# Values of layer 1 weighed three key tiles at a time behind every sixth pair, with sixteen weight buffers

## What is computed

```python
q, k, v = proj(wq, bq), proj(wk, bk), proj(wv, bv)
scores = einsum("bhqd,bhkd->bhqk", q, k) / sqrt(16) + spatial_bias_matrix
attn = softmax(scores, axis=-1)
ctx = einsum("bhqk,bhkd->bhqd", attn, v)
resid = ctx.reshape(B, S, 128) @ wo + bo + x_seq
out = layernorm(resid) * ln_gamma + ln_beta
```

## Time and profile before

| | |
|---|---|
| median of 3 runs | 10369.0 us (10361.93 to 10372.07) |
| profiled execution, its own time | 10373.9 us |
| its span | 10372.1 us |
| TensorE matmul busy | 9606.5 us, 93% |
| VectorE busy | 7181.1 us, 69% |
| ScalarE busy | 5674.1 us, 55% |
| GpSimd busy | 963.2 us, 9% |

### The profile page before, as it was taken

One profiled execution on the slowest core, in us unless ns is written; L12 is line 12 of the kernel. 1 busy time (PEld: TensorE's weight loads), 2 busy tenths in 40 slices (PEclk: granted clock), 3 DMA queues, 4 the chain that ended last, 5 costly groups with the idle time before them and its releaser, 6 DMA issues.

```text
span 10372.1 us, 345836 instructions
## 1 busy us (share of the span) xinstructions
PE 9606.5 (93%) x139471; PEld 4590.9 (44%) x139471; DVE 7181.1 (69%) x24584; ACT 5674.1 (55%) x11896; POOL 963.2 (9%) x862
## 2 busy tenths in 40 slices
PE   7888851699999999999999999999999999999998
PEld 4444430244444444444444444444444444444444
DVE  3555540577777777777777777777777777777774
ACT  1111100266666666666666666666666666666665
POOL 0222220100100010001000100011001100110001
PEclk8888875699999999999999999999999999999999
DMA  2444434100110011001100110011001100110000
GB/s 54 86 85 87 85 85 31 49 10 16 35 29 11 14 36 31 11 14 36 32 10 14 34 34 9 15 31 34 11 15 30 29 17 13 33 28 19 10 13 15
DMA packets 443040, 324.25 MB, mean 31 GB/s; under 512 B 75495, under 2 KB 436424, under 8 KB 440520
## 3 DMA queue, kind: packets, MB, share of 16 engines
q1 hardware_dynamic: 433988, 299.91, 12.5%
q10 hardware_dynamic: 7488, 2.77, 0.5%
HBM read 197.66 MB, written 104.87 MB: 29 GB/s over the span
## 4 chain that ended last, share of the span: by engine, by line
PE 75%; ACT 3%; DMA 2%; SPq 1%; issue 1%; DVE 0%; POOL 0%; ACTq 0%; POOLq 0%; DVEq 0%
PE l_ps L1006 51%; PE l_ps L1084 22%; ACT p L1187 2%; DMA sums_scratch<-ctx_raw 1%; PE l_ps L1099 1%; PE l_ps L1115 1%; ACT rows L1179 1%; PE l_ps L1116 0%; PE l_ps L1102 0%; SPq L842 0%; DMA sums<-sums_scratch 0%; PE l_ps L1096 0%; SPq L837 0%; SPq L830 0%; DMA stacks_scratch<-parts 0%
## 5 line engine op out<-in xcount | busy, mean ns | idle before, releaser
L1187 ACT ACTIVATE p<-l_ps 128x448 f32<-128x448 f32 x10976 | 5263.9, 543 | 2691.4 <-PE l_ps L1006 2683.9
L1228 DVE CUSTOM_DVE_ANT_0 summed<-l_ps,pair_bias 128x448 f16<-128x448 f32 x9408 | 5379.8, 619 | 1792.0 <-PE l_ps L1006 1776.2
L1006 PE MATMUL l_ps<-ks,qs 64*64 64x448 f16 x21952 | 3925.8, 355 | 59.3 <-DVE partial L1228 35.0
L1006 PE MATMUL l_ps<-high,id 64*64 64x448 f16 x21952 | 3928.9, 354 | 27.6 <-ACT p L1187 3.0
L1006 PE MATMUL l_ps<-qs,ks 64*64 64x448 f16 x21952 | 3922.7, 354 | 0.0
L1006 PE MATMUL l_ps<-low,id 64*64 64x448 f16 x21952 | 3902.4, 352 | 0.7 <-issue 0.7
L1006 PE MATMUL l_ps<-rows,pick_row 64*64 64x448 f16 x21952 | 3874.2, 349 | 0.0
L1084 PE MATMUL l_ps<-p,v 128*32 128x448 f32 x22400 | 2413.9, 547 | 0.0
L1006 PEld LDWEIGHTS l_ps<-high,id 64*64 64x64 f16 x21952 | 1204.1, 106 | 1493.8 <-issue 981.0
L1006 PEld LDWEIGHTS l_ps<-ks,qs 64*64 64x64 f16 x21952 | 1204.1, 106 | 877.0 <-DVE partial L1228 573.6
L1006 PEld LDWEIGHTS l_ps<-qs,ks 64*64 64x64 f16 x21952 | 1205.6, 106 | 394.0 <-issue 0.4
(11 more groups left out here) (130 smaller groups left out, 4285.7 us busy)
## 6 DMA issues: line engine op xcount, KB each, us to landing
stacks_scratch<-parts SPq DMA_DIRECT2D x448, 112.0 KB
x<-in_x SPq DMA_DIRECT2D x16, 1568.0 KB
ks<-stacks_scratch SPq DMA_DIRECT2D x32, 784.0 KB, 9.6
qs<-stacks_scratch SPq DMA_DIRECT2D x224, 112.0 KB, 2.8
recip<-inverse_scratch SPq DMA_DIRECT2D x448, 56.0 KB, 2.0
h_scratch<-x SPq DMA_DIRECT2D x8, 1568.0 KB
w_scratch<-x SPq DMA_DIRECT2D x8, 1568.0 KB
mh<-h_scratch SPq DMA_DIRECT2D x64, 196.0 KB
```

The costliest lines, as they stand in the source:

```text
L1006: last = nc.tensor.matmul(ps[h * BT:(h + 1) * BT, bank, 0:CH], lhs(part, h), rhs(part, h), start=start, stop=True, skip_group_check=not start)
L1187: nc.scalar.activation(p[unit % PB][:], ps[:, bank_of(unit), 0:CH], ACT.Exp).then_inc(exp_done, 1)
L1228: nc.vector.tensor_tensor_reduce(summed[unit % 2][:], ps[:, AB + unit % MAXIMA, 0:CH], bias.rearrange("p s t -> p (s t)"), 1.0, LOWEST, AL ...
```

## The change

`PB` goes from 12 to 16, and `weighed_at` names other pairs: three key tiles behind pairs 7, 13, 19, ... 43 and behind pair 0 of the next tile, and the last key tile behind pair 2 as before. The products, the exponentials, the maxima and the DMAs are the same in number and in shape.

```diff
-        PB = 12
+        PB = 16
...
             if i == 0 and n >= 1:
-                return [(n - 1, 22), (n - 1, 23)]
+                return [(n - 1, 21), (n - 1, 22), (n - 1, 23)]
             if i == 2 and n >= 1:
                 return [(n - 1, 24)]
-            if i % 4 == 1 and i >= 5 and 0 <= n < N:
-                return [(n, i // 4 * 2 - 2), (n, i // 4 * 2 - 1)]
+            if i % 6 == 1 and i >= 7 and 0 <= n < N:
+                return [(n, i // 6 * 3 - 3), (n, i // 6 * 3 - 2), (n, i // 6 * 3 - 1)]
```

## The result

| | before | with the change |
|---|---|---|
| median | 10367.6 us (10361.9 to 10372.1, 4 runs) | 10539.6 us (10535.6 to 10540.8, 4 runs) |
| profiled execution, its span | 10372.1 us | 10538.3 us |
| granted clock, mean | 0.95 | 0.95 |

The change makes the kernel slower: ratio 1.0166, 95% interval [1.0148, 1.0183], 172 us. The forecast was 10520 us in a range of 10450 to 10585.

A forecast was written before the change was run, and what follows sets the result against it. TensorE sets the time, but VectorE is slower while pairs run. 56 tiles at +1.35 and 56 at +1.78 us make 175; less 31, plus 9, less 2 gives +151: 10520 us, range 10450 to 10585.

The forecast's parts named there:

- What bounds: Between weighings TensorE (0.943 us a pair) outruns VectorE (1.09); four pairs is just where the three banks run out.
- Fewer blocks, -0.93 a tile: Weighing blocks on TensorE: fewer, longer blocks save 1.64 us, free stretches grow by 0.71; sum -0.93 us per query tile.
- the 0.25 of the rows side: Before the change, the stretch with the rows side is 0.25 us too long; with the change a block covers it.
- Longer stretches, +1.86: Pairs between weighings: each further pair costs VectorE's 1.09 us; six pairs take 5.86, not 5.49; +1.86 us per tile.
- `join`, +0.42 net: VectorE's `join` behind pair 39 (0.80 us) falls mid-stretch, no longer hidden: +0.67, less 0.25 for the rows side.
- Layer norm, +0.43: In half of the tiles, norm work on VectorE lengthens bound stretches: 3.75 us against 3.32 before, +0.43 a tile.
- Projection pieces, -31 us: 196 pieces between pairs, in norm tiles, give VectorE time and clear 0.16 us each: -31 us, bounds nothing and -73.
- Reciprocal that waits, +9 us: Some 14 times VectorE is held by a transfer behind a key load; the gain of fewer blocks there is lost.
- At nothing: ScalarE's pace, weighing's waits for exponentials, the 16 buffers, DMAs and SyncE's order: no effect; last 58 pairs 2 us less.
- Only the turns count: Rival: TensorE saves 448 turns between tilings, waits for VectorE stay: -104 us, 10265, chance 0.05.
- Only the plain part is felt: Rival: banks run out, but `join` and norm stay hidden behind weighing and pieces: +82 us, 10450, chance 0.17.
- More than the pace: Rival: each held TensorE step also restarts slower, 0.38 in place of 0.35 us: 72 us more, 10590, chance 0.15.

## Why the prediction was right, point by point

The sum fell short by 19 us of 170. By tiles, those with a load of keys were put 16 us too low and those with pieces 9, the plain ones and those with norm only 3 each too high. The misses partly cancel, so that the total came out as near as it did is in part luck.

- *What bounds.* Right and shown: the halved maxima turn the sign of the change, and the held steps begin at 3.68 us of a stretch, where the sum had them.
- *Fewer blocks, -0.93 a tile.* Right, and a little too small. A block of three is 2.70 in the median (2.72 forecast), one of four 3.45: a further key tile costs 0.75 and not 0.77. With 1.94 for a block of two the blocks save 1.73 a tile and not 1.64; with VectorE out of the way the changed order's plain tile is 1.15 shorter, where 0.93 and the 0.25 of the rows side were due.
- *Longer stretches, +1.86.* Right: six pairs 5.86, as forecast, eight pairs 8.04.
- *`join`, +0.42 net.* Right in mechanism and size: 5.58 for the five pairs where 4.77 + 0.80 was summed, and moving it away gave 73 us, where 0.67 in 112 tiles is 75. A plain tile came to +1.27 where +1.35 was summed; the blocks make that 0.08.
- *Layer norm, +0.43.* Too much: tiles with norm only came to 1.5 to 1.6 more, not 1.78. From block to block such a tile lies over a plain one by 2.73 (pairs 26 to 31, 2.75 summed), 0.59 (32 to 37, for 0.65), 0.14 (38 to 43, for 0.21) and 0.14 (as summed). So it is the small steps that were put too high, at 0.07 each without a row of their own.
- *Projection pieces, -31 us.* 9 us too favourable: 37 us in 35 tiles, where 28 x 1.78 + 7 x 1.35 - 31 = 28 was summed (7 of the 35 have no norm).
- *Reciprocal that waits, +9 us.* **The mis-sized term.** The tiles with a load of keys make 51 us, where the other terms and this one gave 14 x 1.78 + 1.35 + 9 = 35. As tiles with norm and without such a wait they would make 14 x 1.53 + 1.3 = 23, so 28 us are this term's. Three things are in them. VectorE reaches the reciprocal 0.64 us earlier (in a tile without a wait it starts 12.55 us behind the last key tile's weighing before, 11.91 now): over 14 tiles these are the 9 us that were summed, the gain of fewer blocks lost in the wait. The sums land later, which I had taken as fixed: 15.16 to 15.73 us behind the weighing in the two reciprocals shown (the earlier trace rows and 5071.46 above, weighings at 4998.10 and 5055.73), 15.55 to 16.19 in the mean of the 14, 9 us more. Where that comes from in SyncE's queue was not tried. With these two the waits go from 40.8 to 58.8 us. And the clock falls behind the longer stalls, estimated at 11 us more than before; the sum had no such term.
- *At nothing.* Right for the buffers (ratio 1.0001) and for the wait on exponentials (328.8 against 306.3 us). That the clock stays the same holds for the mean (0.95) and for plain stretches, not behind the 14 stalls.
- *The rivals.* "Only the turns count" is out in this kernel and true with short maxima. "Only the plain part is felt" (10450) is out: `join` and norm were felt. "More than the pace" (10590) is out: in a bound stretch the distances are 1.09 and nothing more.

My expectations for two later runs failed by the same neglect: I treated the cost of other work as fixed and not as a matter of its place between blocks (eight pairs), or did not ask what the first block of a tile waits for (two pairs).

## What to carry to other kernels

When a producer alternates between work that feeds a consumer and work that doesn't, compare the paces inside the feeding phase, not the busy shares: the banks between them hide the difference for so many units, and every unit beyond costs the consumer's pace. Past the point where the banks run out, fewer switches may save less than the longer phase costs; here, of two, four, six and eight pairs, four was best, which is where three banks ran out. And all other work of the consumer belongs directly ahead of the phase that doesn't feed it; whoever moves the phases must move that work with them, which was worth more here (over 1%) than the number of phases (0.8%).

## What the runs showed of the hardware

A turn from quarters of the array to strips and back costs TensorE 0.22 to 0.25 us beside the steps themselves, whether one, two, three or four key tiles stand between (medians 1.17, 1.94, 2.70 and 3.45 us from score step to score step, less 0.75 per key tile and 0.19 for a step). A VectorE reduction from accumulator memory over 224 in place of 448 columns takes 0.37 in place of 0.545 us from start to start, so about 0.2 us of it do not depend on the columns; I had expected 0.3. (The split is an estimate from these two lengths.) The granted clock was 0.50, the lower level, 1.2 GHz, behind a stall in which TensorE had started nothing for 3.55 us; a step of four score products then took 0.37 in place of 0.19 us.
